# Self-attention of a decoder layer: full products against 64x64 quarter tiles

## The reference, cut to what matters

```
xn  = layernorm(x) * g1
q   = xn @ Wq.T                # 16 heads of 64
k,v = split(xn @ Wkv.T)        # one head of 64 each, shared by all query heads
q,k = l2norm(q * 16) * 4, l2norm(k) * 4
sim = q @ k.T, causal mask
out = softmax(sim) @ v         # per head
y   = layernorm(out @ Wout.T) * g2
x   = layernorm(x + y)
```

## Time and profile before

| | |
|---|---|
| three runs | 885.01, 885.24, 880.82 us, median 885.01 |
| profiled execution | 882.52 us, of which the span is 880.8 us |
| PE, PEld busy | 783.5 us (89%), 654.3 us (74%) |
| DVE, ACT, POOL busy | 632.1 (72%), 593.7 (67%), 452.0 us (51%) |
| mean granted clock of TensorE | 0.981 |
| first and last start of `x_T` (L1498) | 7.5 and 290.4 us |
| first and last start of `normalise` (L970) | 20.1 and 305.0 us |

### The profile page before, as it was taken

The page is one execution under the profiler, slowest core; times in us unless marked ns, Lnnn a source line. Parts: engine busy times, 40 slices in busy tenths (PEclk is TensorE's granted clock), DMA queues, the critical chain, the costliest instruction groups (busy, mean ns, idle before and its releaser), DMA issues.

```text
span 880.8 us, 26463 instructions
## 1 busy us (share of the span) xinstructions
PE 783.5 (89%) x9205; PEld 654.3 (74%) x9237; DVE 632.1 (72%) x1898; ACT 593.7 (67%) x1444; POOL 452.0 (51%) x440
## 2 busy tenths in 40 slices
PE   4799999999999988999999999999997877687776
PEld 3577777778787767888888878788886767677752
DVE  3878778878787757778787878788888555445425
ACT  2677878888787856777676767777766454455535
POOL 5477676776767632223535353535342545554443
PEclk9899999999999999999999999999999999889998
DMA  8499999000000000000000000000002455556636
GB/s 282 82 157 161 158 156 121 2 0 0 0 0 0 2 1 6 7 7 7 27 10 28 10 28 9 24 13 25 12 22 73 136 166 175 159 177 184 204 104 231
DMA packets 69505, 65.30 MB, mean 74 GB/s; under 512 B 5689, under 2 KB 54972, under 8 KB 69280
## 3 DMA queue, kind: packets, MB, share of 16 engines
q1 hardware_dynamic: 62592, 51.42, 28.5%
q0 software_dynamic: 4736, 10.12, 3.3%
q10 hardware_dynamic: 2080, 2.49, 0.9%
HBM read 35.88 MB, written 28.58 MB: 73 GB/s over the span
## 4 chain that ended last, share of the span: by engine, by line
PE 51%; issue 20%; POOL 12%; ACT 6%; DVE 6%; DMA 3%; another core or an unknown queue 1%; SPq 1%; POOLq 0%; ACTq 0%; DVEq 0%
PE bank L1791 7%; PE bank L1687 7%; PE bank L1487 6%; PE bank L1489 5%; PE bank L1488 5%; POOL rq L530 5%; PE bank L1662 3%; PE bank L1675 3%; POOL PR L535 3%; PE bank L1801 3%; PE bank L1563 2%; PE bank L1571 2%; ACT VBD L391 2%; PE bank L1781 1%; POOL rs L544 1%
## 5 line engine op out<-in xcount | busy, mean ns | idle before, releaser
L391 ACT COPY VBD<-bank 64x512 f32<-64x512 f32 x192 | 111.2, 579 | 28.5 <-PE bank L1489 25.8
L567 POOL TENSOR_TENSOR PR<-PR,rL 128x1024 f32<-128x1024 f32 x32 | 60.9, 1902 | 115.7 <-DVE rL L1114 115.6
L530 POOL TENSOR_TENSOR rq<-ssq,mhalf 128x17 f32<-128x17 f32 x32 | 99.2, 3100 | 15.7 <-DVE ssq L963 15.1
L627 POOL DMA_INDIRECT zbuf<-PT,KT x71 | 69.8, 983 | 72.3 <-ACT PT L889 50.2
L535 POOL TENSOR_TENSOR PR<-PR,rL 128x1024 f32<-128x1024 f32 x32 | 60.9, 1904 | 82.4 <-DVE rL L994 82.4
L1417 DVE SCALAR_TENSOR_TENSOR stage<-bank,b_now,early 128x128 f32<-128x128 f32 x142 | 43.1, 345 | 61.9 <-ACT early L881 46.2
L1791 PE MATMUL bank<-xT,w_now 128*128 128x128 f32 x568 | 82.7, 292 | 0.4 <-DMA w_now<-in_wl 0.3
L619 POOL DMA_INDIRECT xbuf<-xg,slot x64 | 64.9, 1014 | 34.3 <-DVE xg L1283 21.8
L881 ACT ACTIVATE early<-bank,b_now 128x128 f32<-128x128 f32 x142 | 44.4, 367 | 56.3 <-PE bank L1791 38.4
L1791 PEld LDWEIGHTS bank<-xT,w_now 128*128 128x128 f32 x568 | 73.8, 203 | 1.6 <-issue 1.3
L797 ACT ACTIVATE PT<-bank 128x512 f32<-128x512 f32 x64 | 38.3, 600 | 43.3 <-PE bank L1675 41.5
(11 more groups left out here) (243 smaller groups left out, 2338.8 us busy)
## 6 DMA issues: line engine op xcount, KB each, us to landing
w_now<-in_wl SPq DMA_DIRECT2D x71, 256.0 KB
xbuf<-blank SPq DMA_DIRECT2D x1, 17160.0 KB, 120.5
KT<-xbuf SPq DMA_DIRECT2D x71, 65.0 KB
VBD<-zbuf SPq DMA_DIRECT2D x4, 512.0 KB, 5.1
out<-X SPq DMA_DIRECT2D x8, 256.0 KB, 2.3
cT<-in_ctxT ACTq DMA_DIRECT2D x16, 96.0 KB, 2.0
zbuf<-PT,KT POOLq DMA_INDIRECT x71
wl_sb<-in_wl POOLq DMA_DIRECT2D x1, 1024.0 KB, 9.3
```

Source lines behind the costliest of these rows:

```text
L391: u = copy(VBD[h * SEQ:(h + 1) * SEQ, p, s, lo:lo + blocks, :], bank[CHUNK_BANK[c]][s * SEQ:(s + 1) * SEQ, :].rearrange("k (a d) -> k a d" ...
L530: nc.gpsimd.tensor_tensor(rq[:, :], ssq[:, :], mhalf[:, 0:HEADS + 1], ALU.pow).then_inc(a["pow"], 1)
L567: nc.gpsimd.tensor_tensor(v, v, rL[:, p, :].unsqueeze(2).broadcast_to([P, HEADS, SEQ]), ALU.mult)\
L627: nc.gpsimd.indirect_dma_start(out=zbuf, out_offset=at, in_=yb[:, t % YB, :], in_offset=None, bounds_check=K2 * TOK - 1, oob_is_err=False) ...
```

## The change

Four products are recast into tiles of the array, and what they need is laid out anew.

- Mask: instead of two products of a 128x128 identity, four of 64x64, one for each quarter (row half h, column half s).
- Values: instead of two products of block-diagonal 128x128 weights, four of 64x64, one for each half of keys and each sequence. The outputs of h = 0 go to bank 4, of h = 1 to bank 5, and the half of bank that a sequence goes to is swapped for h = 1.
- For that the values must lie on both halves of the partitions: PE makes the keys with one product of 64 columns, and the values with four products of 128x64 weights and 64 columns. ACT copies keys and values (192 columns) to kvS and later the values to vS; `k_norm` reads kvS and not bank 1. The two `v_bd` stages and the zeroing of VBD are gone; ACT's `v_keep` stands in the place of its `v_bd`.
- Projection: because of the swapped halves, each of the eight products of K = 128 becomes four of 64x64, two into bank 0 and two into bank 1 (columns 256 to 383), with a second copy of the weights, wout_swap, whose halves are exchanged. ACT copies bank 0 to yA, and a new DVE stage `y_take` adds bank 1 to it and writes yS. It is called in DVE's body right behind `sums`.
- Waits: as bank 1 is shared now, `x_T` and `qkv` in PE's stream wait for kvS, oT and yS in place of other stages' waits.

```
 # act
-nc.scalar.activation(vS[:, p, :], bank[1][:, DH:2 * DH], ACT.Copy).then_inc(a["vS"], 1)
+nc.scalar.activation(kvS[:, p, :], bank[1][:, 0:(1 + PB) * DH], ACT.Copy).then_inc(a["kvS"], 1)
...
-def v_bd(t, p): ...            # two copies of 64x64
+def v_keep(t, p):
+    act.wait_ge(a["kvS"], t + 1)
+    nc.scalar.activation(vS[:, p, :, :]..., kvS[:, p, DH:(1 + PB) * DH], ACT.Copy).then_inc(a["vS"], 1)
...
 def y_evac(t, p):
-    nc.scalar.activation(yS[:, :], bank[0][:, 0:D], ACT.Copy).then_inc(a["yS"], 1)
+    nc.scalar.activation(yA[:, :], bank[0][:, 0:D], ACT.Copy).then_inc(a["yA"], 1)
 # dve
-def v_bd(t, p): ...            # two copies of 64x64
+def y_take(t, p):
+    dve.wait_ge(a["yA"], t + 1)
+    if later(t, 1):
+        dve.wait_ge(a["yn"], t)
+    V.tensor_tensor(yS[:, :], bank[1][:, 2 * D:3 * D], yA[:, :], ALU.add).then_inc(a["yS"], 1)
...
 stage_of(sums, i, p, 0)
+stage_of(y_take, i, p, 3)
 stage_of(ln_var, i, p, -2)
 # pe, x_T
+if not isinstance(t, int):
+    pe.wait_ge(a["kvS"], t); pe.wait_ge(a["oT"], 2 * (t - 3)); pe.wait_ge(a["yS"], t - 4)
 # pe, qkv
-M(bank[1][:, 0:2 * DH], xT[:, p, :], wkv_sb[:, :], start=True, stop=True).then_inc(a["kv"], 1)
+M(bank[1][:, 0:DH], xT[:, p, :], wkv_sb[:, 0:DH], start=True, stop=True)
+for s in range(PB):
+    for h in range(2):
+        m = M(bank[1][h * DH:(h + 1) * DH, (1 + s) * DH:(2 + s) * DH], xT[:, p, s * SEQ:(s + 1) * SEQ],
+              wkv_sb[:, DH:2 * DH], start=True, stop=True)
+m.then_inc(a["kv"], 1)
 # pe, scores
 for h in range(2):
-    M(bank[6 + h][:, :], ident_b[:, :], causal[:, :, :]..., start=True, stop=False)
+    r = slice(h * DH, (h + 1) * DH)
+    for s in range(PB):
+        M(bank[6 + h][s * SEQ:(s + 1) * SEQ, :], ident_b[r, r], causal[r, :, :]..., start=True, stop=False)
 # pe, values
-M(bank[4 + s][:, :], VBD[:, p, s, 0, :], PT[:, s * HW:(s + 1) * HW], start=True, stop=True)
+for s in range(PB):
+    for h in range(2):
+        r = slice(h * DH, (h + 1) * DH)
+        half = s if h == 0 else 1 - s
+        m = M(bank[4 + h][half * DH:(half + 1) * DH, :], vS[r, p, s, :], PT[r, s * HW:(s + 1) * HW], start=True, stop=True)
 # pe, project, for each of 8 k
-m = M(bank[0][:, 0:D], OT[:, k, :], wout_sb[:, k, :], start=(k == 0), stop=(k == NBLK - 1))
+M(bank[0][0:SEQ, 0:D], OT[lo, k, even], wout_sb[lo, k, :], **g)
+m0 = M(bank[0][SEQ:P, 0:D], OT[lo, k, odd], wout_swap[lo, k, :], **g)
+M(bank[1][0:SEQ, 2 * D:3 * D], OT[hi, k, odd], wout_sb[hi, k, :], **g)
+m1 = M(bank[1][SEQ:P, 2 * D:3 * D], OT[hi, k, even], wout_swap[hi, k, :], **g)
 # sp, behind the load of wout_sb
+sp.dma_start(wout_swap[0:DH, :, :], woutT[DH:P, :, :]).then_inc(w_out, 16)
+sp.dma_start(wout_swap[DH:P, :, :], woutT[0:DH, :, :]).then_inc(w_out, 16)
```

More of the change, by code:

```diff
@@ L690, in k_norm @@
                     act.wait_ge(a["knT"], t)
-                nc.scalar.activation(kn[:, :, :], bank[1][:, 0:DH].unsqueeze(1).broadcast_to([P, PB, DH]), ACT.Copy,
+                act.wait_ge(a["kvS"], t + 1)
+                nc.scalar.activation(kn[:, :, :], kvS[:, p, 0:DH].unsqueeze(1).broadcast_to([P, PB, DH]), ACT.Copy,
                                      scale=rinv[:, HEADS:HEADS + 1]).then_inc(a["kn"], 1)
-            def v_bd(t, p):
-                act.wait_ge(a["vS"], t + 1)
+            def v_keep(t, p):
+                act.wait_ge(a["kvS"], t + 1)
                 if later(t, 2):
                     act.wait_ge(a["o"], 2 * (t - 1))
-                for h in range(2):
-                    v = nc.scalar.copy(VBD[h * DH:(h + 1) * DH, p, 1, 0, h * DH:(h + 1) * DH], vS[SEQ:2 * SEQ, p, :])
-                v.then_inc(a["v1"], 1)
+                nc.scalar.activation(vS[:, p, :, :].rearrange("k s d -> k (s d)"), kvS[:, p, DH:(1 + PB) * DH], ACT.Copy)\
+                  .then_inc(a["vS"], 1)
             def exp_half(t, p, c):
@@ L736, in _ @@
             act.wait_ge(w_in, 32)
-            act.wait_ge(zeroed, 1)
             def body(i, p):
@@ L979, in normalise @@
                      .then_inc(a["qn"], 1)
[L981 to L987, removed]
             def softmax(t, p):
@@ L1493, in x_T @@
                 pe.wait_ge(a["xn"], t + 1)
+                if not isinstance(t, int):
+                    pe.wait_ge(a["kvS"], t)
+                    pe.wait_ge(a["oT"], 2 * (t - 3))
+                    pe.wait_ge(a["yS"], t - 4)
                 if later(t, 1):
@@ L1557, in p_T, with values @@
                 m.then_inc(a["pT_ps"], 1)
-            def values(t, p, s):
+            def values(t, p):
+                pe.wait_ge(consts, 11)
                 pe.wait_ge(a["pT"], 2 * (t + 1))
[L1561 to L1564, removed]
-            def project(t, p):
-                pe.wait_ge(a["oT"], 2 * (t + 1))
-                if later(t, 1):
-                    pe.wait_ge(a["yS"], t)
-                for k in range(NBLK):
-                    m = M(bank[0][:, 0:D], OT[:, k, :], wout_sb[:, k, :], start=(k == 0), stop=(k == NBLK - 1))
-                m.then_inc(a["y"], 1)
+                pe.wait_ge(a["vS"], t + 1)
+                for s in range(PB):
+                    for h in range(2):
+                        r = slice(h * DH, (h + 1) * DH)
+                        half = s if h == 0 else 1 - s
+                        m = M(bank[4 + h][half * DH:(half + 1) * DH, :], vS[r, p, s, :], PT[r, s * HW:(s + 1) * HW],
+                              start=True, stop=True)
+                        if s == PB - 1:
+                            m.then_inc(a["o"], 1)
+            def project(t, p):
+                if isinstance(t, int):
+                    pe.wait_ge(a["oT"], 2 * (t + 1))
+                    pe.wait_ge(a["kvS"], min(t + 4, T))
+                    if t >= 1:
+                        pe.wait_ge(a["yS"], t)
+                if isinstance(t, int) and t == T - 3:
+                    pe.wait_ge(b["xlo"], 2)
+                lo, hi = slice(0, DH), slice(DH, P)
+                even, odd = slice(0, SEQ), slice(SEQ, 2 * SEQ)
+                for k in range(NBLK):
+                    g = dict(start=(k == 0), stop=(k == NBLK - 1))
+                    M(bank[0][0:SEQ, 0:D], OT[lo, k, even], wout_sb[lo, k, :], **g)
+                    m0 = M(bank[0][SEQ:P, 0:D], OT[lo, k, odd], wout_swap[lo, k, :], **g)
+                    M(bank[1][0:SEQ, 2 * D:3 * D], OT[hi, k, odd], wout_sb[hi, k, :], **g)
+                    m1 = M(bank[1][SEQ:P, 2 * D:3 * D], OT[hi, k, even], wout_swap[hi, k, :], **g)
+                m0.then_inc(a["y"], 1)
+                m1.then_inc(a["y"], 1)
             pe.wait_ge(consts, 11)
@@ L1763, in cross @@
                     project(T - 2, 0)
-                    for c in range(2):
-                        values(T - 1, 1, c)
+                    values(T - 1, 1)
                     project(T - 1, 1)
-            pe.wait_ge(a["kn"], T)
+            pe.wait_ge(a["kvS"], T)
+            pe.wait_ge(a["yS"], T - 3)
             bx_T(0, 0)
```

43 lines of the change are left out of this document (23 added, 20 removed).

## The result

The changed kernel takes 925.0 us (median of four runs, 923.98 to 930.54), the kernel before, run beside it, 884.9: a ratio of 1.048 (95% interval 1.043 to 1.053). The medians are 40 us apart, the ratio of all the runs makes it 42. The forecast was 890.5, with 876 to 900 as the range. The profiled execution took 925.47 us, its span is 923.7; mean granted clock 0.968.

The account below looks back on a forecast made before the run. A ring through projection, y_take and DVE's work was to set the period, 9.3 against 9.08 us; 882.52 + 7.0 + 0.5 = 890.0, predicted as 890.5 because the profiled execution lies below the median; range 876 to 900.

Parts of the forecast that it names:

- Ring C: Loop of qkv, projection, y_evac, y_take, DVE's shadow work, L970, L976: 9.22 and 9.45 us, setting the period, +0.25 a tile.
- The keys and values: PE's new products for keys and values, with changes of tile shape in and out: +0.55 us a tile.
- Part by part, PE: PE's work per tile, summed over values, mask, keys and values, projection and shape changes: from 8.81 to 8.57 us.
- Rival 3: Quarters of 512 or 128 columns don't overlap on PE: work 9.6 us or more a tile, 899 us; chance 0.10.
- Rival 4: Issue bounds PE's projection, 64 records at 62 ns each: +2.2 us a tile, 945 us; chance 0.01.
- Rival 1: Kernel gets faster, as additions ahead of PE's projection stay under 0.3 us a tile: 876 us; chance 0.20.
- Rival 2: Half and half: additions of about 0.3 us ahead of the projection, no change in time, 884 us; chance 0.22.
- S: Start of `qkv` in a tile on PE, 0.75 us behind the start of L976; reference point for the projection's copy.
- there are 28 periods: +7.0 us: From tile 3 to tile 31, each of 28 periods costs 0.25 us more, 7.0 us in total.
- the chain's PE-only stretch: Unrolled bodies where the chain of waits is PE alone: 8.81 us between L1563 starts, taken as PE's own work per tile.
- The ends: Start of the kernel and behind body 31: together +0.5 us net, between -1 and +2.

Follow-up runs that it names:

- run 2: Changed kernel with the 17 MB fill issued after PE's q of tile 10 and y_take moved later in DVE's queue, just ahead of y_stats: 875.1 us, ratio 0.991.
- run 5: Changed kernel with only y_take moved later in DVE's queue, just ahead of y_stats, the fill in its old place: 911.1 us, ratio 1.032.
- run 1: Changed kernel with one edit, the 17 MB fill of xbuf issued only once PE has made q of tile 10: 893.0 us, ratio 1.010.
- run 3: Kernel before the change, with the 17 MB fill issued only once PE has made q of tile 10: 881.4 us, ratio 0.9985.
- run 7: Kernel before with the late fill and DVE's two v_bd copies given to ACT, no quarter tiles: 875.0 us, ratio 0.991.
- run 9: Also e9: kernel before, fill in its old place, 60 small products added in each of seven written-out bodies: 906.3 us, ratio 1.031.

## Why the prediction was wrong

**Ring C: right, term by term.** Forecast 9.22 and 9.45, measured 9.19 and 9.45. The step from the copy of the projection to L994 is 0.31 in this tile and 0.40 in the next (forecast 0.32), the next instruction starts 0.21 later (0.21), L940 to L1009 take 1.91 (1.92), then 0.26, 0.30 and 0.74 (0.26, 0.30, 0.75). The keys and values cost PE 0.64 us from L1517 to L1531, where L1511 took 0.22: +0.42, forecast +0.55; the copy of the projection still came where I put it, since the other small terms ahead of it were together a tenth more than forecast. Two small misses cancel there. Runs 2 and 5 show that it is a ring: with `y_take` further back in DVE's queue, 8.74 remain.

**Part by part, PE: the tiles right.** Two rounds of the projection in the changed kernel, each with three more quarters beside it:

```profile
212.13 0.27 PE L1599 MATMUL bank<-arena 64*64 64x128 f32 x1
...
212.24 0.27 PE L1599 MATMUL bank<-arena 64*64 64x128 f32 x1
```

The values' eight records take 1.03 us (two rounds of 0.43 and the end), the mask's four go in one round, 0.24 ahead of the scores. Rivals 3 and 4 are out: quarters of 512 columns run four at once, and the projection's rounds follow by 0.11 us, as forecast. Rivals 1 and 2 are out too, as the additions ahead of the projection moved its copy by the forecast 0.55 us (5.45 and 5.56 behind S, before 4.91 and 4.99).

**The step that failed: "there are 28 periods: +7.0 us".** The 28 periods cost 39.3 us more, not 7.0: 35.5 in the seven from tile 3 to tile 10, and 4.5 in the nineteen from there to tile 29, for which 0.25 each makes 4.8. The step gives every tile, in the loop or written out, the loop's period, and prices added PE instructions by the array's time alone. For the tiles that PE runs from code still coming in, an instruction has another price, which the forecast never asked for: 124 more in a tile, 35.5 us in all over tiles 3 to 10, of which ring C is about 2 (64.4 in run 1 against 62.5 in run 3). The trace of before held a hint: under the fill its periods from tile 3 to tile 10 are 8.9 to 9.6 us, where the late fill gives 8.6 to 9.1, and a code queue had seven transfers from 40 to 160 us and none from 160 to 280. I took the chain's PE-only stretch for PE's own work, which run 7 bears out, and did not look at what else PE lived on there. Rival 4 asked for the price of issue and priced it by the time that each record would take to issue, in every tile alike; it needed to be asked for the written-out tiles, and by the supply of their code. That is a mechanism missing, not a term mis-sized.

The Trainium skill, Runtime: NRT & Kernel Launch, section Instruction fetch mechanics, says that PE's code comes in blocks of 16 KiB, fetched ahead by a DMA queue of its own, and calls the cost of crossing a block "mostly hidden". The block agrees with the page of the profile (1.05 MB in 64 transfers, 16.4 KB each); "hidden" holds in run 1 and not under the fill, where the same ten transfers between 40 and 160 us go with a time 32 us longer.

**The ends: under-priced.** They cost 3.6 us, forecast +0.5 with a bound of +2. Tile 3 starts 2.1 us later: 1.5 of it is the period ahead of it, 10.15 for 8.63, where `y_take` holds DVE for the first time (run 2 has 8.51 there). Behind tile 31 it is +1.5. The spans of runs 1 and 3 (893.6 and 878.9) are 14.7 apart, a little more than their medians: 3.1 up to the start of tile 3, 5.9 from there to tile 31, 5.6 behind it; why more behind it than in the changed kernel I can't say. One profiled execution of each kernel stands behind these splits, and executions of one kernel differ by some 4 us.

**What stays open.** Why code comes so slowly under this fill. It is not the transfers themselves: by the view of the DMA queues one takes 1.2 to 1.9 us under the fill and 0.9 to 1.4 in run 1. In the changed kernel they start 9 to 13.5 us apart under the fill, in run 1 as close as 3.5, so the time goes before a transfer starts. The fill's writes are small (some 33,000 packets of 520 bytes), so it may be their number and not their bytes; no run here varies that.

## What to carry to other kernels

Before adding many small instructions to an engine, split its timeline in two: where it loops and where it runs written-out code, and in the second divide the instructions by the microseconds. If the engine stands there with no releaser while a large transfer is under way, and its stops end behind transfers of the code queue, the code's supply is the bound, and further instructions are paid nearly in full: 840 of them cost 25 us in run 9. Move the transfer, or start the loop earlier. And where a wait is put into a queue ahead of work that needed no wait, place it at its latest harmless position: that was worth 18 us here with the fill moved and 14 without, and the work that it had been added for was worth nothing measurable.

## What the runs showed of the hardware

- PE's code came at 22 to 26 instructions per us (438, 510 and 489 records in 40 us in the changed kernel and e9, each with a load) while a fill moved 160 GB/s, and at 39 or more (776 records in 40 us) without it.
- A loop of two tiles fetched next to no code: one transfer in q8 from 160 to 280 us in the changed kernel, none before and in run 1. It ran at its usual rate under the same fill (768 records in 40 us in run 1).
- Four 64x64 quarters of 512 float32 columns run at once: eight records in 1.03 us, where four of 128x128 took 1.98.
- Standing for code cost clock too: the granted clock in the windows above is 0.91 and 0.89 where PE stood, 0.80 in e9, and 1.00 where it did not. It fell right behind a stop: in e9 PE stood for 5.9 us until 81.2, and from 80 to 85 us the clock is 0.50, the level of 1.2 GHz. Behind the stop that ends at 67.08 in the changed kernel, seven of the values' records take 1.92 us, where all eight take 1.03 at 2.4 GHz.
